# Fifty TensorE products whose results nobody reads, taken out of a two-layer perceiver kernel

## What is computed

```python
x = x + _L0_xattn_ref(_layernorm(x), ctx_512, Wq, Wkv_expand, Wout)    # causal cross attention, 32 keys, 16 heads of 16
x = x + _L0_attn_ref(_layernorm(x), g_norm, Wq, Wkv, Wout, g_out)      # 16 heads of 128, one shared key and value head
x = x + _L0_ffn_ref(_layernorm(x), Wr, br, W1, W2)                     # 16 blocks of 64, each token uses its best 4
x = x + _L1_xattn_ref(_layernorm(x), ctx_512, Wq, w_kc_q, w_kc_kv, W_qr, W_kr, Wo)  # latent attention over 257 keys
x = x + _L1_attn_ref(_layernorm(x), Wq, bq, Wk, bk, Wv, bv)            # causal, 4 key groups of 16 heads
x = x + _L1_ffn_ref(_layernorm(x), router_w, gate_w, up_w, down_w)     # 8 experts, each token goes to its best one
```

## Time and profile before

| | |
|---|---|
| median of 3 runs | 1154.27 us (1152.2 to 1154.68) |
| the profiled execution's own time | 1154.21 us |
| its span, first to last instruction | 1152.4 us |
| TensorE busy | 1087.5 us, 94% of the span |
| VectorE / ScalarE / GpSimd busy | 708.1 / 452.3 / 301.6 us |
| mean granted clock of TensorE | 0.978 of full speed |

### The profile page before, as it was taken

How to read it: one execution, slowest core, us unless ns; L and a number is a source line. 1 busy time by engine, 2 the same in 40 slices (tenths; PEclk the granted TensorE clock), 3 DMA queues, 4 the chain that set the end, 5 groups by cost and what they waited for, 6 DMA issues and landing times. The chain is left out here.

```text
span 1152.4 us, 32210 instructions
## 1 busy us (share of the span) xinstructions
PE 1087.5 (94%) x12466; PEld 830.2 (72%) x12467; DVE 708.1 (61%) x1806; ACT 452.3 (39%) x1329; POOL 301.6 (26%) x390
## 2 busy tenths in 40 slices
PE   7898999999999999999979999999998799899996
PEld 6676878888778768989756766776766588556664
DVE  6898754554646475646547888888885687422221
ACT  2453443434435222221145555555553565222221
POOL 1701523323131200000001221221214535234442
PEclk9899999999999999999989999999999998799998
DMA  8631211111121119000202323333244633312211
GB/s 266 173 89 36 71 46 49 43 39 55 27 55 27 37 35 253 1 0 0 57 1 70 92 75 78 77 84 76 70 139 145 200 77 100 84 30 35 35 27 11
DMA packets 72655, 82.56 MB, mean 72 GB/s; under 512 B 28942, under 2 KB 57263, under 8 KB 72140
## 3 DMA queue, kind: packets, MB, share of 16 engines
q1 hardware_dynamic: 64284, 62.33, 20.4%
q0 software_dynamic: 8304, 19.32, 6.4%
HBM read 64.91 MB, written 18.53 MB: 72 GB/s over the span
## 5 line engine op out<-in xcount | busy, mean ns | idle before, releaser
L1780 ACT ACTIVATE xattn_exps<-xattn_ps_s,xattn_top 128x256 f32<-128x256 f32 x256 | 117.8, 474 | 84.7 <-DVE xattn_top L1844 84.7
L777 PEld LDWEIGHTS attn_ps_q<-attn_xnT,w_b_q 128*128 128x128 f32 x1024 | 120.0, 194 | 12.6 <-issue 12.6
L777 PE MATMUL attn_ps_q<-attn_xnT,w_b_q 128*128 128x128 f32 x1024 | 124.6, 278 | 0.0
L831 PE MATMUL attn_ps_out<-w_b_o,attn_oT 128*128 128x256 f32 x480 | 106.6, 380 | 2.6 <-DVE all_x L1012 1.5
L831 PEld LDWEIGHTS attn_ps_out<-w_b_o,attn_oT 128*128 128x128 f32 x480 | 90.0, 190 | 16.1 <-DVE all_x L1012 2.4
L885 ACT COPY attn_qT<-attn_ps_q 128x512 f32<-128x512 f32 x64 | 38.1, 595 | 148.7 <-PE attn_ps_q L777 148.7
L1851 DVE STREAM_TRANSPOSE xattn_expsT<-xattn_exps 128x1024 f32<-128x1024 f32 x64 | 79.5, 1242 | 26.4 <-ACT xattn_exps L1780 26.3
L1841 DVE TENSOR_REDUCE xattn_raw_top<-xattn_ps_s 128x4 f32<-128x1024 f32 x64 | 77.3, 1208 | 14.7 <-PE xattn_ps_s L1671 14.2
L1648 PEld LDWEIGHTS xattn_ps_o<-xattn_xnT,all_d_a 128*128 128x128 f32 x512 | 61.9, 198 | 17.9 <-ACT xattn_exps L1780 7.2
L1613 POOL TENSOR_TENSOR xattn_ctxT<-xattn_weighed_sum,xattn_inverse 128x256 f32<-128x256 f32 x60 | 41.9, 730 | 125.3 <-DMA xattn_inverse<-xattn_inverse_rows 125.3
L1671 PE MATMUL xattn_ps_s<-all_c,xattn_qT 64*32 64x256 f32 x2048 | 69.8, 382 | 2.8 <-ACT xattn_exps L1780 2.8
(11 more groups left out here) (361 smaller groups left out, 2214.7 us busy)
## 6 DMA issues: line engine op xcount, KB each, us to landing
all_c<-roped_kT SPq DMA_DIRECT2D x32, 256.0 KB, 3.9
xattn_inverse<-xattn_inverse_rows SPq DMA_DIRECT2D x30, 256.0 KB, 4.0
attn_k_raw<-in_ctx SPq DMA_DIRECT2D x64, 64.0 KB, 1.9
roped_kv<-attn_k_kv SPq DMA_DIRECT2D x16, 256.0 KB, 2.1
roped_kT<-attn_k_turned SPq DMA_DIRECT2D x64, 64.0 KB, 1.7
all_c<-roped_kv SPq DMA_DIRECT2D x16, 256.0 KB, 2.9
moe_gate<-in_f_gate SPq DMA_DIRECT2D x8, 512.0 KB, 8.2
moe_up<-in_f_up POOLq DMA_DIRECT2D x8, 512.0 KB, 5.2
```

What stands on the lines that cost most here:

```text
L777: last = nc.tensor.matmul(ps_q[g % 2][:, h * P:(h + 1) * P], wq[:, c, head * DH:(head + 1) * DH], xnT[u][:, c, :], start=(c == 0), stop=(c ...
L831: last = nc.tensor.matmul(bank[:, 0:DIM], of_heads[:, h, :, :].rearrange("p b q -> p (b q)"), wo[:, h, :], start=(h == 0), stop=(h == HEAD ...
L1780: nc.scalar.activation(exps[g % 2][:, nkeys * k:nkeys * (k + 1)], ps_s[g % 2][:, nkeys * k:nkeys * (k + 1)], ACT.Exp, bias=top[u][:, n:n + ...
```

## The change

The helper `keep_busy` and all its calls are deleted, in all five blocks that had it. That is 50 products (22 of 256 columns, 28 of 512), or 100 matmul records. Two pieces of the same kind stay, since they are not written through the helper: two products at the end of `small_attention` (L455) and one at the end of `latent_attention` (L1770). Nothing else is edited; the waits that stood behind a removed product now stand at the next product.

```diff
-            def keep_busy(products):
-                for n in range(products):
-                    nc.tensor.matmul(ps_o[:, 0:DIM], ident, consts[:, 0:DIM], start=True, stop=True)
-
-            keep_busy(10 if cross else 2)
...
                 if cross and late:
                     finish(i - 2, TILES)
-                if cross and isinstance(i, int) and i < 1:
-                    keep_busy(4)
...
-            def keep_busy(products, bank=ps_out):
-                for n in range(products):
-                    nc.tensor.matmul(bank[:, :], ident, consts[:, 0:512], start=True, stop=True)
-
-            keep_busy(1)
...
                 if isinstance(i, int) and i == TILES - 1:
-                    keep_busy(2, ps_q[1])
                     finish(i - 1, range(0, 10))
...
             run_steps(pe, step, -2, TILES - 1, 2, TILES - 3)
-            keep_busy(5, ps_q[1])
...
             def step(i, u, live):
-                if isinstance(i, int) and i == TILES:
-                    keep_busy(2, ps_h[0])
...
-            keep_busy(1)
             run_steps(pe, step, -1, TILES, 2, TILES - 2)
...
                         pe.wait_ge(s["sum_ready"], TB * t)
-                        keep_busy(4)
                         pe.wait_ge(s["exps_ready"], per_group * (groups * t + 3))
...
-            keep_busy(1, ps_o[:, :])
             for semaphore, n in loaded:
...
             pe.wait_ge(s["scores_out"], TILES)
-            keep_busy(2, ps_g[0])
...
             last.then_inc(s["ranked"], 1)
-            keep_busy(6, ps_g[0])
...
             last.then_inc(s["token_made"], 1)
-            keep_busy(4, ps_g[0])
```

More of the change, by code:

```diff
@@ L1691, in weigh_tail @@
                     last.then_inc(s["weighed"], 1)
-            def keep_busy(products):
-                for n in range(products):
-                    nc.tensor.matmul(ps_turn[:, :], ident, consts[:, 0:512], start=True, stop=True)
             def spread_inverse():
@@ L2150, in _ @@
             mm = nc.tensor.matmul
-            def keep_busy(products, bank):
-                for n in range(products):
-                    mm(bank, ident, consts[:, 0:512], start=True, stop=True)
-            keep_busy(1, ps_o[:, :])
             for semaphore, n in loaded:
```

3 lines of the change are left out of this document (removed).

## The result

The changed kernel took 1158.66 us, median of 20 runs (1155.16 to 1164.47), against 1153.96 us for the kernel before, 20 runs beside them (1149.23 to 1168.28). The ratio is 1.004, with a 95% interval of 1.0023 to 1.0058: +4.7 us (2.7 to 6.7). It is slower, as forecast, and the time lies in the forecast's range, but the change costs 4.7 us where the forecast's sum had 9.7.

A forecast was written before the change was run, and what follows sets the result against it. TensorE, busy 94% of the span, was taken to bound the kernel, at two clock levels. Eight terms summed to +9.7 us on 1154.21, giving 1163.9 us; most likely 1160 to 1168, or 1157.5 to 1169.5 with two rivals included.

The forecast's parts named there:

- (a): Start of the first stage, 22 products: less queueing against a slower clock, +1.0 us net (bounds -2.9 and +4).
- (b): Start of shared_key_attention, one product: TensorE could begin the turning 0.2 us earlier, -0.2 us (bounds -0.3 and +1).
- (c): Last step of shared_key_attention, two products: 3.4 us idle, clock falls, output product late, +2.2 us (1.6 to 2.8).
- (d): End of shared_key_attention and start of block_routed_ffn, five products and one: 5.6 us gap, clock falls, +2.1 us (1.2 to 2.8).
- (e): Last step of block_routed_ffn, two products: idle gap of 1.8 us, taken as 0; +2 us if the clock falls.
- (f): Last tile of latent_attention, four products: 3.7 us gap, clock falls, output product slow, +2.2 us (1.6 to 2.8).
- (g): Start of the last attention, one product: clock falls, first tile's chain runs low, +1.5 us (bounds 0 and 2.8).
- (h): Routing, twelve products from 988.1 to 1002.9 us: clock stays low all through, +0.9 us (0 to 2.2).
- the price of a dip: TensorE work lost in one stretch at the low clock level: 1.6 to 2.8 us, 2.2 in the mean.
- The rival that the clock holds: Whole kernel: no new low-clock stretches, only queueing given back, 4.1 us at most, about 1150 us; chance 0.05.
- the rise at 9.5 us: Sign in the first stage: with its products removed, the clock would no longer rise at 9.5 us.

The follow-up runs named there:

- e8: Kernel before without the unread products of (a), (b), (g) and (h) together: 1152.46 us against 1152.63, ratio 1.0008 (0.9982 to 1.0035).
- e11: Kernel before without the unread products of (e), (f) and (g) together: 1151.18 us against 1152.45, ratio 0.9998 (0.9969 to 1.0026).

## Why the prediction was right in direction and too high

By its own steps, with what each kernel that has the edit (removed) and each that doesn't (kept) showed on VectorE's lag:

```
term  forecast  lag, removed                          lag, kept      by time, where tried
(a)   +1.0      mean +1.4 at 114 us (6 profiles)      +1.3 (10)      +0.8 (-1.4 to +3.1)
(b)   -0.2      +0.5                                  +0.2           in e8
(c)   +2.2      +2.6 +1.5 +2.0 +2.6 +2.5              0 each time    +3.0 (0.1 to 5.8)
(d)   +2.1      +2.2 +3.3 +2.2 +2.1 +2.1              0 each time    +3.6 (0.7 to 6.4)
(e)    0        0, +1.7, 0, 0, 0                      0              in e11, -0.2
(f)   +2.2      +2.7 +3.3 -0.3 +1.0 0.0 +2.7          -0.2           +0.5 (-2.3 to +3.2)
(g)   +1.5      +1.6                                  +0.9           in e8, e11
(h)   +0.9      +0.6                                  +0.2           +1.4 (-1.5 to +4.3)
```

**What was right.** The view that decided was the one by windows, and the price of a dip taken from it, 1.6 to 2.8 us, held: (c) measured 2.2 in the mean of five profiles for a forecast of 2.2, (d) 2.4 for 2.1. The rival that the clock holds is out. In (a) the first query block came 1.3 us earlier, the number that the prediction gave, and the rise at 9.5 us was absent: the first tile's queries took 2.07 us where the earlier trace rows has 1.16.

```profile
10.12 0.66 PE L333 MATMUL xattn_ps_T<-all_consts,xattn_xn 128*128 128x128 f32 x2 [10.12 <-DVE xattn_xn L152]
...
12.66 2.07 PE L359 MATMUL xattn_ps_q<-xattn_xnT,w_a_q 128*128 128x128 f32 x8
```

**The steps that failed are (g) and (h), as terms of the sum; (g) first.** It read "Without it ... the clock falls" and compared with a profile in which the clock had held through gaps of 0.3 and 1.74 us. With the product in place it fell in seven of eleven profiles, without it in six of six. So the edit costs only where the clock would have held, 0.8 us in the mean. And the next stretch, which waits for values from DMA, gives back about as much: there the lag changes by -2.3 in the mean without (g) and by -1.1 with it, though single profiles lie between +0.6 and -3.4. Nothing of the +1.5 can be seen at the end. The prediction had named the other ground, that transfers may hide it, as a bound of 0; it should have asked first whether the product holds the clock at all.

**(h) failed in the same manner.** The low stretch without a break up to the first experts came as described, though it began at 988 and not at 972 as in before's profile. But TensorE is busy for only 14.38 us of those 30, and 6.6 of them belong to the loop, up to 994.58, where the clock falls with the wide products too. The rest stands beside work that sets the pace: 18.45 us from loop to experts against 18.1. What was priced as clock was waiting for VectorE and the gather. Between 1005 and 1013 the lag grows by 0.4 us more without the products than with them; between 965 and 1005 it grows by 0.5 less, so nothing is left.

**(f) was taken for certain and isn't.** The clock fell fully behind gaps of 3.41, 3.52 and 4.18 us, late in the product behind one of 3.15 (5.25 us for it), and not behind gaps of 3.31 and 3.63. The changed kernel in its second profile, the kernel without (e), (f) and (g), and the changed kernel in its third:

```profile
872.19 6.44 PE L1690 MATMUL xattn_ps_s<-all_d_b,xattn_ctxT 128*128 128x256 f32 x16 [4.18 <-POOL xattn_ctxT L1595]
```

```profile
862.42 5.25 PE L1709 MATMUL xattn_ps_s<-all_d_b,xattn_ctxT 128*128 128x256 f32 x16 [3.15 <-POOL xattn_ctxT L1611]
```

```profile
868.55 3.69 PE L1690 MATMUL xattn_ps_s<-all_d_b,xattn_ctxT 128*128 128x256 f32 x16 [3.63 <-POOL xattn_ctxT L1595]
```

The last has a longer gap than the first profile's 3.41 us, and full speed. So the length of the gap alone doesn't decide. The prediction's "one of 3 us has brought the level down wherever this trace has one" rested on few cases: the trace of before has gaps of 3.19, 2.92 and 2.96 us with a fall in or just behind them (at 28.5, 110.9 and 584.2 us), and it also has one of 2.76 us, at 598.2, through which the clock held; the prediction didn't look at that one. Over six profiles the lag grows by 1.6 us, 1.8 more than where the products stand. The clock fell in full in three of four that also lack (a), in neither of the two that keep it, where the lag was +1.0 and -0.3; whether this is chance or the earlier stages shift the later ones is open. The Trainium skill ("TensorE: Matmul & The Clock Gate", section "What's actually happening") says of a kernel's start that the number of slow matmuls there varies from run to run of the same kernel. The two profiles of the changed kernel, 3.41 us and low, 3.63 us and high, show the like in the middle of a kernel, of which the page doesn't speak.

**The sum again.** With 0.1 for (a), 0.3 (b), 2.2 (c), 2.4 (d), 0.3 (e), 1.8 (f) and nothing for (g) and (h), the profiles' parts give +7.1, where the forecast had +9.7. The +1.0 of (a) shrinks because the kernels that keep its products were 1.3 us late at 114 as well: before's profile had one of the quicker first stages. Too large were (g) by 1.5, (h) and (a) by 0.9 each, (f) by 0.4; too small (b) by 0.5, (d) and (e) by 0.3 each. The whole was measured three times: +4.7 (2.7 to 6.7), +11.3 (7.5 to 15.1) and +6.8 us (3.8 to 9.7). The first two intervals don't overlap, so the three scatter more than their intervals allow. Weighted by these the mean is +6.3, give or take 1.5 if they are taken at their word, and about twice that by the scatter of the three; +7.1 agrees with it. So of the 5.0 us between forecast and result, 2.6 are terms of mine that were too large, and 2.4 lie between the parts and the first measurement of the whole, which was the lowest of the three. The second measurement, +11.3, would have the forecast's +9.7 inside its interval: how much too high the sum was is known less well than that (g) and (h) were.

Two slips of the prediction's arithmetic changed nothing: the queueing in (a) is 2.2 + 0.9 = 3.1 us and not 2.9, and the lower bounds of the terms add to +1.2 and not to about +2.

**What the runs don't settle.** Single terms under 3 us are at the edge of what five rounds tell; (a) to (h) are sized by profiles, one execution each. That the time of one execution goes with its clock is better founded: over the 29 to 35 runs of the kernel before in each session of experiments, time and mean granted clock have a correlation of -0.8 to -0.9, and 0.001 of clock goes with 0.9 to 1.05 us. The whole change takes 0.014 from the clock. By that line it would cost 12 to 15 us; it costs about half. The routing is a part of the reason: (h) alone took 0.005 of the clock, by the line 4 to 5 us, and cost 1.4 (-1.5 to 4.3), since there TensorE is waited for by nobody most of the time.

The Trainium skill ("TensorE: Matmul & The Clock Gate", section "What's actually happening") holds that for modelling the ramp is under 1% of a typical span. The runs' mean clock is 0.979 before and 0.965 after, 2.1% and 3.5% short of full, so the trace doesn't agree with that as a size. The prediction read from the rule that the time couldn't be far above 1160, and it was 1158.66. That is luck: 1% of the span is 11.5 us, added to 1154.2 it allows 1165.7, so the rule doesn't part the result from my 1163.9, and its premise didn't hold here.

## What to carry over

A product that nobody reads is worth its place only where three things hold: TensorE would idle there, the work behind it is TensorE's own and on the path, and the clock stays up with it and falls without it. The third has to be read from several executions, with the product and without, since one profile may show the clock held or lost by luck. And what a stage gains by its clock should be followed to its next transfer: here a stage that was 2.2 us ahead waited 3.91 us there and lost 5.8 in all, though the same wait came in three executions without the fill.

## What the runs showed of the hardware that I had not expected

- The first stage varies from one execution to the next, with the same code: in four executions, three of them without an edit in that stage, the weighted sum waited 3.07 to 5.41 us for its value blocks and the stage ended 3.6 to 5.0 us late; in before's profile the same wait was 0.52 us, and in the others it was at most 2.73.
- At one place of one kernel a gap of 3.63 us left the clock up and one of 3.41 us did not, and behind the last attention's 1.75 us the clock fell in 13 of 17 profiles, with a wide product ahead of it (7 of 11) or without (6 of 6).
- Most of the spread between executions of one kernel, 1144 to 1165 us for the kernel before in the sessions of the experiments, goes with its mean granted clock.
